# A two-layer gated cross-attention kernel: the first head's keys and queries laid out by TensorE instead of by way of memory, and the mask summed by GpSimd inside the loop

## The reference, cut to what matters

```
x = x + tanh(g_xattn[0]) * attention0(layernorm(x), ctx)        # 16 heads of 8 channels, no mask
x = x + tanh(g_ffn[0])   * top-2 gated experts0(layernorm(x))   # 8 experts, gelu
x = x + tanh(g_xattn[1]) * attention1(ctx, layernorm(x), mask)  # 16 heads, mask
x = x + tanh(g_ffn[1])   * top-2 gated experts1(layernorm(x))   # 8 experts, silu gate
```

## Time and profile before

| what | value |
|---|---|
| median of 3 runs | 2676.83 us (2675.81 to 2679.16) |
| the profiled execution's own time | 2674.73 us |
| its span, first to last instruction | 2672.7 us |
| mean granted TensorE clock in it | 0.949 |
| TensorE busy / VectorE / ScalarE / GpSimd | 93% / 81% / 72% / 1% |
| first max unit's reduction starts at | 74.37 us |
| the loop over the first head's steps starts at | 195.16 us |

### The profile page before, as it was taken

The page is one execution under the profiler, slowest core; times in us unless marked ns, Lnnn a source line. Parts: engine busy times, 40 slices in busy tenths (PEclk is TensorE's granted clock), DMA queues, the critical chain, the costliest instruction groups (busy, mean ns, idle before and its releaser), DMA issues.

```text
span 2672.7 us, 50522 instructions
## 1 busy us (share of the span) xinstructions
PE 2493.9 (93%) x20890; PEld 952.0 (36%) x20892; DVE 2156.5 (81%) x2215; ACT 1935.6 (72%) x3545; POOL 27.6 (1%) x27
## 2 busy tenths in 40 slices
PE   2379999999999999999796899999999999999989
PEld 1243333333333333334342333333333333333343
DVE  5469999999999999953536899999999999999144
ACT  2058888888888888885331388888888888888932
POOL 4000000000000000000000000000000000000000
PEclk8559999999999999999896799999999999999989
DMA  7120000000000000003100000000000000000000
GB/s 251 69 82 21 29 29 29 29 29 29 29 28 28 28 29 29 23 24 109 65 0 22 6 29 28 28 28 28 29 29 29 29 29 28 28 28 14 1 0 8
DMA packets 36415, 94.33 MB, mean 35 GB/s; under 512 B 4020, under 2 KB 14808, under 8 KB 35928
## 3 DMA queue, kind: packets, MB, share of 16 engines
q1 hardware_dynamic: 34744, 90.69, 9.4%
q10 hardware_dynamic: 1440, 0.40, 0.1%
HBM read 75.08 MB, written 15.74 MB: 34 GB/s over the span
## 4 chain that ended last, share of the span: by engine, by line
PE 63%; DVE 31%; SPq 2%; DMA 1%; issue 1%; ACT 1%; DVEq 0%; ACTq 0%
DVE m_part L657 28%; PE ps L978 22%; PE ps L930 19%; PE ps L949 10%; PE ps L1076 4%; PE ps L1084 3%; SPq L299 1%; PE ps L890 1%; PE ps L920 1%; DMA probs<-in_mask_t 1%; PE ps L882 1%; DVE probs L613 1%; SPq L308 1%; PE ps L1096 1%; DMA k_parts<-probs 1%
## 5 line engine op out<-in xcount | busy, mean ns | idle before, releaser
L657 DVE TENSOR_REDUCE m_part<-ps 128x2 f32<-128x1024 f32 (+1 forms) x1664 | 1932.5, 1184 | 166.9 <-PE ps L949 162.3
L495 ACT ACTIVATE probs<-ps 128x512 f32<-128x512 f32 (+1 forms) x3264 | 1759.5, 595 | 314.3 <-PE ps L930 194.9
L978 PE MATMUL ps<-probs,v_all 128*9 128x256 f32 x13056 | 1013.0, 382 | 1.7 <-ACT o_raw L475 0.5
L930 PE MATMUL ps<-q_ring,k_ring 35*128 35x512 f32 x3264 | 872.6, 497 | 0.6 <-ACT q_ring L484 0.4
L949 PE MATMUL ps<-k_ring,q_ring 33*128 33x512 f32 (+1 forms) x3328 | 732.3, 419 | 62.5 <-DVE m_part L657 36.2
L930 PEld LDWEIGHTS ps<-q_ring,k_ring 35*128 35x128 f32 x3264 | 347.9, 183 | 712.9 <-ACT probs L495 618.3
L949 PEld LDWEIGHTS ps<-k_ring,q_ring 33*128 33x128 f32 x3328 | 348.9, 193 | 150.6 <-DVE m_part L657 108.7
L978 PEld LDWEIGHTS ps<-probs,v_all 128*9 128x9 f32 x13056 | 194.4, 88 | 551.5 <-ACT probs L495 472.8
L794 DVE TENSOR_TENSOR probs<-probs,ps 128x512 f32<-128x512 f32 x64 | 39.7, 683 | 74.5 <-ACT probs L528 70.1
L528 ACT ACTIVATE probs<-ps,b_col 128x512 f32<-128x512 f32 x64 | 44.0, 687 | 70.2 <-PE ps L1076 70.2
L678 DVE RECIPROCAL r_den<-ps 128x8 f32<-128x8 f32 x32 | 6.6, 207 | 107.0 <-PE ps L957 106.7
(11 more groups left out here) (127 smaller groups left out, 576.1 us busy)
## 6 DMA issues: line engine op xcount, KB each, us to landing
k_ring<-k_parts SPq DMA_DIRECT2D x384, 96.0 KB
k_ring<-k_parts SPq DMA_DIRECT2D x128, 112.2 KB
probs<-in_mask_t SPq DMA_DIRECT2D x10, 640.0 KB, 4.4
k_parts<-probs SPq DMA_DIRECT2D x12, 512.0 KB, 3.1
k_parts<-big SPq DMA_DIRECT2D x12, 512.0 KB, 3.1
q_ring<-q_parts SPq DMA_DIRECT2D x120, 32.0 KB
big<-in_w SPq DMA_DIRECT2D x1, 2048.0 KB, 10.7
q_parts<-probs SPq DMA_DIRECT2D x4, 512.0 KB, 3.5
```

The costliest lines, as they stand in the source:

```text
L495: A(probs[0:k, n % PSLOTS, HALF * half:HALF * half + HALF], ps[0:k, e_bank(unit), :], ACT.Exp, scale=SCALE).then_inc(sem(f"exp_done{l}"), 1)
L657: V.tensor_reduce(m_part[:, h % 2, :, p, c], mx(n % 2)[:, :, 0:chunk_w[c]], AX.X, ALU.max).then_inc(sem(f"mx_done{l}"), 1)
L930: pe.matmul(bank, k_ring[row:row + ROWS_EXP, koff:koff + P], q_ring[row:row + ROWS_EXP, qoff:qoff + HALF], start=not masked, stop=True).th ...
L978: mm = pe.matmul(ps[32 * g:32 * g + VW, 7, 0:QGW], v_all[:, t, h, :], probs[:, n % PSLOTS, QGW * g:QGW * g + QGW], start=(t == 0), stop=(t ...
```

## The change

- **The first head, layer 0.** Its rows no longer come through memory. After a chunk's keys are projected and split, TensorE multiplies them with two small selection matrices (`repeat`), which puts the 8 channels on their 64 rows of a PSUM bank, and ScalarE copies that bank into `k_ring` and adds the ones by a bias column (`copy_over`). The queries go the same way, with four matmuls. Three chunks are projected ahead; the other ten are projected between the first head's own max units, as are the repeats.
- **Who splits.** ScalarE evacuates each key chunk twice (rounded, and as it is), and GpSimd forms the low part (`low_keys`), not VectorE. `k_st` and `q_st` of layer 0 now lie in the second slot of `k_ring`.
- **The mask.** GpSimd adds the 11 pieces as 32-bit words (`put_mask_together`) after its work on the keys; VectorE reduces the folded remainder before layer 1. ScalarE's `sum_mask` is gone, and the stage has moved to the `spare` part of `big`.
- **SyncE's queue.** Order: x, ctx, queries' store, key stores 0 to 2, queries of head 1, key group 0 of head 1, the other key stores, key groups 1 to 3 of head 1 (after all 14 copies), queries of head 2, then `setup`, then `check_mask`, then `load_heads`. The first head's eight query and sixteen key transfers are gone.
- **GpSimd's start.** The long memsets are gone from it: selection matrices first, then (after the layer norm) short memsets, `low_keys`, the constants that VectorE waits for (`rank`) after the third chunk, and the ones of the second slot in two parts (`set_ones`).
- **Small things.** The rows unit is a matmul by a rounded identity, not a transpose; `keep_warm` runs four times in each of the two steps before the first `weigh`, and the dense steps are eight, not four, in both layers; one buffer for the row biases; the values have one PSUM bank and stand one unit earlier; one table function (tanh) moved behind the first maxima.

The diff, cut to its core:

```diff
 def dense(h, t):
 
-    return 3 if h == 0 and t < 4 else 0
+    return 3 if h == 0 and t < 8 else 0
 K_GROUPS = [(0, 3), (3, 6), (6, 9), (9, KCH)]
+UPPER = 6
+
+
+REPEATS = [0, "q"] + list(range(1, KCH))
+REPEAT_AT = {u: n for n, u in enumerate(REPEATS)}
+RING_SET = KRING + 2
+MASK_LEFT = 160
...
-        k_st = [of[:, 0:KST * PARTS * HALF].bitcast(F32R).rearrange("p (a b w) -> p a b w", a=KST, b=PARTS)
-                for of in (flat3(probs)[:, 2 * TQ:], spare)]
+        sum_stage = [spare[:, n * MCH * TQ // 4:(n + 1) * MCH * TQ // 4] for n in range(2)]
+        k_st = [of[:, 0:KST * PARTS * HALF].rearrange("p (a b w) -> p a b w", a=KST, b=PARTS)
+                for of in (k_ring[:, KW + HALF * UPPER:], spare.bitcast(F32R))]
+        mask_sum = spare[:, KST * PARTS * HALF:KST * PARTS * HALF + MCH * TQ // 4]
+        k_sum = spare[:, TQ:2 * TQ].rearrange("p (a w) -> p a w", a=2)
+        r_at = KW + 2 * PARTS * HALF
+        r_k = k_ring[0:HD, r_at:r_at + PARTS * P].rearrange("p (n r) -> p n r", n=PARTS)
+        r_q = k_ring[0:HD, r_at + PARTS * P:r_at + 3 * PARTS * P].rearrange("p (n r) -> p n r", n=2 * PARTS)
...
             def load_first0():
 
-                sp.wait_ge(sem("ring_set"), RING_SET)
-                first_queries(0)
-                store_k(0)
+                store_q(0)
+                for g, (c0, c1) in enumerate(K_GROUPS):
+                    store_k(0, c0, c1)
+                    if g == 0:
+                        sp.wait_ge(sem("ring_set"), RING_SET)
+                        sp.wait_ge(sem("q_stored0"), 16 * 2)
+                        load_queries(0, 1)
+                        sp.wait_ge(sem("copied_over"), REPEAT_AT["q"] + 1)
+                        keys_stored(0, c1)
+                        load_keys(0, 1, g)
                 keys_stored(0)
-                for g in range(len(K_GROUPS)):
-                    load_keys(0, 0, g)
-                sp.wait_ge(sem("q_stored0"), 16 * 2)
-                load_queries(0, 1)
-                for g in range(len(K_GROUPS)):
+                sp.wait_ge(sem("copied_over"), NCH + 1)
+                for g in range(1, len(K_GROUPS)):
                     load_keys(0, 1, g)
                 load_queries(0, 2)
...
             sp.dma_start(x_sb[:, :, :], a["x"].rearrange("(t p) c -> p t c", p=P)).then_inc(sem("x_in"), 16)
+            load_context()
+            load_first0()
             setup()
-            load_first0()
             check_mask()
...
+                selections()
+                pool.wait_ge(sem("xn_q0"), QT)
                 set_ring()
+
+            def more_constants():
+                link(nc.gpsimd.tensor_scalar(neg_i[:, :], ident_f[:, :], MASKED, 0.0, ALU.mult, ALU.add))
+                link(nc.gpsimd.memset(m_pad[:, :, :].bitcast(F32), 0.0))
+                link(nc.gpsimd.memset(ones_f[:, :], 1.0))
                 for e in range(E):
-                    nc.gpsimd.memset(rank[:, e:e + 1], float(E - e)).then_inc(sem("rank"), 1)
-                nc.gpsimd.memset(ones_f[:, :], 1.0).then_inc(sem("rank"), 1)
-                nc.gpsimd.memset(m_pad[:, :, :], 0.0).then_inc(sem("rank"), 1)
+                    link(nc.gpsimd.memset(rank[:, e:e + 1], float(E - e)))
                 nc.gpsimd.memset(zeros[:, :], 0.0).then_inc(sem("rank"), 1)
-                nc.gpsimd.tensor_scalar(neg_i[:, :], ident_f[:, :], MASKED, 0.0, ALU.mult, ALU.add).then_inc(sem("rank"), 1)
-                pool.wait_ge(sem("rank"), E + 4)
+                pool.wait_ge(sem("rank"), 1)
                 nc.gpsimd.tensor_tensor(pick_e[:, :], ident_f[0:2 * E, 0:E], ident_f[0:2 * E, E:2 * E], ALU.add).then_inc(sem("pick_e"), 1)
+                pool.wait_ge(sem("pick_e"), 1)
+                nc.gpsimd.tensor_scalar(ident_r[:, :], ident_f[:, :], 1.0, 0.0, ALU.mult, ALU.add).then_inc(sem("ident_r"), 1)
+                pool.wait_ge(sem("ident_r"), 1)
```

```diff
+            def low_keys(c):
+
+                w = chunk_w[c]
+                pool.wait_ge(sem("k_evac0"), 2 * c + 2)
+                nc.gpsimd.tensor_tensor(k_st[0][:, c % KST, 1, 0:w], k_sum[:, c % 2, 0:w], k_st[0][:, c % KST, 0, 0:w].bitcast(F32),
+                                        ALU.subtract).then_inc(sem("k_split0"), 1)
+                pool.wait_ge(sem("k_split0"), c + 1)
+
+            def put_mask_together():
+
+                words = mask_sum.bitcast(I32)
+                link(nc.gpsimd.memset(mask_sum, 0.0))
+                for c in range(NFULL // MCH + 1):
+                    pool.wait_ge(sem(f"mask_in{c % 2}"), 16 * (c // 2 + 1))
+                    rows, n = (P, MCH * TQ // 4) if c < NFULL // MCH else (TAIL, TQ // 4)
+                    new = sum_stage[c % 2].bitcast(I32)[0:rows, 0:n]
+                    if c:
+                        pool.wait_ge(sem("mask_met"), c)
+                    nc.gpsimd.tensor_tensor(words[0:rows, 0:n], words[0:rows, 0:n], new, ALU.add).then_inc(sem("mask_met"), 1)
+                pool.wait_ge(sem("mask_met"), NFULL // MCH + 1)
+                n = MCH * TQ // 8
+                while n > MASK_LEFT:
+                    link(nc.gpsimd.tensor_tensor(words[:, 0:n], words[:, 0:n], words[:, n:2 * n], ALU.add))
+                    n //= 2
+                nc.gpsimd.tensor_tensor(words[:, 0:n], words[:, 0:n], words[:, n:2 * n], ALU.add).then_inc(sem("mask_folded"), 1)
 
             constants()
+            for c in range(NCH):
+                low_keys(c)
+                if c == 2:
+                    more_constants()
+                if c == UPPER:
+                    pool.wait_ge(sem("copied_over"), REPEAT_AT["q"] + 1)
+                    pool.wait_ge(sem("q_stored0"), 16 * 2)
+                    set_ones(0, HALF * UPPER, 0)
+            pool.wait_ge(sem("copied_over"), NCH + 1)
+            for n in range(KST):
+                pool.wait_ge(sem(f"k_stored0_{n}"), 16 * len(range(n, NCH, KST)))
+            set_ones(HALF * UPPER, TK, 2)
+            put_mask_together()
...
+            def project_k(c):
+
+                w = chunk_w[c]
+                act.wait_ge(sem("k_proj0"), c + 1)
+                if c >= KST:
+                    act.wait_ge(sem(f"k_stored0_{c % KST}"), 16 * (c // KST))
+                    act.wait_ge(sem("repeated"), REPEAT_AT[c - KST] + 1)
+                A(k_st[0][:, c % KST, 0, 0:w], ps[:, 4 + c % 2, 0:w], ACT.Identity, bias=b_col[:, 0, 1:2]).then_inc(sem("k_evac0"), 1)
+                if c >= 2:
+                    act.wait_ge(sem("k_split0"), c - 1)
+                A(k_sum[:, c % 2, 0:w], ps[:, 4 + c % 2, 0:w], ACT.Identity, bias=b_col[:, 0, 1:2]).then_inc(sem("k_evac0"), 1)
+
+            def copy_over(what):
+
+                act.wait_ge(sem("repeated"), REPEAT_AT[what] + 1)
+                if what == "q":
+                    act.wait_ge(sem("ring_set"), RING_SET)
+                    A(q_ring[:, 0:HALF], ps[:, 6, :], ACT.Identity).then_inc(sem("copied_over"), 1)
+                else:
+                    act.wait_ge(sem("one_rows"), 2)
+                    A(k_ring[:, HALF * what:HALF * what + chunk_w[what]], ps[:, 6, 0:chunk_w[what]], ACT.Identity,
+                      bias=one_rows[:, 0:1]).then_inc(sem("copied_over"), 1)
...
+            project_k(0)
+            project_k(1)
+            project_q(0)
+            copy_over(0)
+            project_k(2)
+            copy_over("q")
+            copy_over(1)
+            for c in range(NCH):
+                if c + 3 < NCH:
+                    project_k(c + 3)
+                if c + 2 < NCH:
+                    copy_over(c + 2)
+                set_v(c)
             act.wait_ge(sem("g_in"), 32)
             A(g_tanh[:, :], g_raw[:, :], ACT.Tanh).then_inc(sem("g_tanh"), 1)
-            act.wait_ge(sem("att_w_in0"), ATT_IN)
-            project_q(0)
-            project_k()
-            for c in range(NCH):
-                set_v(c)
-                if c < NFULL // MCH + 1:
-                    sum_mask(c)
-            act.wait_ge(sem("mask_summed"), NFULL // MCH + 1)
...
                     for c0, _ in CTX_CHUNKS:
                         if c * HALF == c0:
                             pe.wait_ge(sem(f"ctx_in{c0}"), 16)
-                if c >= 2:
-                    pe.wait_ge(sem(f"k_split{l}"), c - 1)
-                pe.matmul(ps[:, c % 2, 0:w], w_att[:, l, 1, :], ctx_t[:, HALF * c:HALF * c + w],
+                if c >= 2 and l == 0:
+                    pe.wait_ge(sem("k_evac0"), 2 * c - 2)
+                if c >= 2 and l == 1:
+                    pe.wait_ge(sem("k_split1"), c - 1)
+                pe.matmul(ps[:, bank + c % 2, 0:w], w_att[:, l, 1, :], ctx_t[:, HALF * c:HALF * c + w],
                           start=True, stop=True).then_inc(sem(f"k_proj{l}"), 1)
```

```diff
+            def repeat(what):
+
+                n = REPEAT_AT[what]
+                pe.wait_ge(sem("selected"), 4 * PARTS)
+                if n:
+                    pe.wait_ge(sem("copied_over"), n)
+                if what == "q":
+                    pe.wait_ge(sem("q_split0"), 2)
```

(58 more changed lines are left out.)

140 lines of the change are left out of this document (70 added, 70 removed).

## The result

The changed kernel took **3258.34 us** (median of 4 runs), the kernel before beside it 2677.99: a ratio of 1.2181, interval 1.2143 to 1.222. Forecast were 2590 us and a range of 2574 to 2624.

A forecast was written before the change was run, and what follows sets the result against it. The page names TensorE, 93% busy, but the first 195 us were read as bound by engines waiting for each other, not arithmetic. Sum: 2674.7 - 89 (earlier loop start) + 8 (queue) - 4 (rows unit) = 2590 us; range 2574 to 2624.

The forecast's parts named there:

- The opening: Layer 0's start up to the first maximum: first reduction at 31 us, before 74.4; range 28 to 36.
- Term 2: The first head's 52 max units in layer 0: 61 us, taking full clock with 3 us lost at the start.
- the half-clock rival: First head's stage: TensorE stays at 1.2 GHz, 87.5 us instead of 61, kernel at 2616 us; chance 0.20.
- the rise at 50 to 54: Old key stage: clock rose from 0.50 to 0.80 behind back-to-back projections; taken as evidence against the half clock.
- the 79%: Old first stage: TensorE said to be 79% busy through 112 us at 0.50; taken as evidence for the half clock.
- Term 3: The eight units of head 1 before the loop: 14 us, 14.6 before; the loop then starts at 106, not 195.
- VectorE was not held by GpSimd: Rival, first stage: GpSimd's low parts and ones hold up VectorE's reductions, 27 us more, 2617 us; chance 0.06.
- Term 4: SyncE's queue: head 2's keys land at +65 against a need at +57 from loop start, a new wait of +8 us.
- slower than before: Rival, SyncE's queue: head 2's keys behind GpSimd's adds; needs a wait above 98 us, 13.6 us per piece; chance 0.02.
- Term 6: The loop's additional keep_warm fillers: cost 2.7 us a layer, return 3 to 4 us by the clock; 0 in sum.
- Term 5: The rows unit in the loop, a one-pass matmul for four transposes: -4 us, ends -8 and +8.

The follow-up runs named there:

- experiment 1: The changed kernel with the mask's pieces queued one behind each head's loads, not all ahead of head 2's keys: 2615.82 us, ratio 0.9753.
- experiment 2: The changed kernel, queue untouched, with three keep_warm in each of seven steps around and behind the wait for head 2's keys: 2628.82 us, ratio 0.98.
- experiment 3: The kernel before with 2 MB weight reloads queued ahead of head 2's keys: three 2673.8 us, three and a half 3318.07, four 3325.88, five 3329.61.
- experiment 8: The changed kernel with the mask's pieces one behind each head's loads and the loop's fillers of before: 2615.14 us, ratio 0.9758.
- experiment 4: The kernel before without any keep_warm fillers in either layer's loop: 3341.22 us, one execution.
- experiment 5: The changed kernel with its wait, and three more keep_warm in each of eight steps of head 3, some 110 steps later: 2721.31 us, one execution.
- Experiment 6: The changed kernel with three keep_warm in steps around the wait, those behind it feeding 9 rows, not 128: 3255.06 us, one execution.
- experiment 9: The changed kernel with mask pieces one behind each head's loads, a full-row matmul in first-stage units, and the loop's old fillers: 2599.25 us, ratio 0.9697.

## Why the prediction was wrong, point by point

**The opening** was right. The changed kernel's timeline (start, us, engine, line, operation):

```profile
7.79 0.17 DVE L718 TENSOR_SCALAR var_e<-mv 128x8 f32<-128x8 f32 x1
...
8.48 2.14 DVE L722 TENSOR_SCALAR probs<-x_sb,mv,r_std 128x128 f32<-128x128 f32 x8
...
14.30 3.54 PE L987 MATMUL ps<-ctx_t,w_att 128*128 128x512 f32 x4 [14.30 <-DMA b_col<-in_bk]
...
32.43 1.23 DVE L762 TENSOR_REDUCE m_part<-ps 128x2 f32<-128x1024 f32 x1 [9.26 <-PE ps L1080]
```

0.17 for 0.2, the weights at 14.30 for 14.2, the first reduction at 32.43 for 31. The lost microsecond and a half is in the first matmuls: the first key chunks took 3.54 us for two where the earlier trace rows have 1.88. That the clock did this is not shown, since the profile reads 1.00 up to 24 us.

**Term 2** took the wrong clock. The 52 units lasted 83.2 us (32.43 to 115.59), near the half-clock rival's 87.5, not 61. I read the rise at 50 to 54 in the earlier trace rows as a sign for the new stage. What stood ahead of that rise was a row of projections of 128 rows; in the new stage such work is thinned out between units of 33. That this is the reason is not shown: the same stage read 1.00 in 64 to 72 and was back at 0.50 from 76 on. Nor did the old stage bear the 79% that I gave it: TensorE was busy 59.16 of the 112 us from 68 to 180, and 78 to 80% only outside its holes. The chunk at half clock is 7.75 us, one period of this timeline:

```profile
45.02 2.07 PE L987 MATMUL ps<-ctx_t,w_att 128*128 128x512 f32 x2
...
47.74 1.22 PE L1005 MATMUL ps<-k_ring 8*128 8x512 f32 x2
...
48.89 1.22 PE L1080 MATMUL ps<-k_ring,q_ring 33*128 33x512 f32 x4
...
50.04 2.07 PE L1014 MATMUL ps<-w_att,ctx_t 128*128 128x128 f32 x8
```

That the stage is bound by TensorE then, at 7.3 us in the text, was right. At full clock the text has 3.7 us of TensorE in a chunk; the trace has TensorE busy 7.72 of 8 us there, and a chunk of 4.83 (values at 64.47 and 69.30). So 61 us would have held at full clock, but with TensorE as full as VectorE. **Term 3** was 15.6 us for 14; the loop starts at 131.17, where the half-clock rival has 132.5. VectorE was not held by GpSimd: its 1.23 us for a maximum stands throughout.

**Term 4** is the step that failed, not in the wait that it foresaw but in what it charged for it. Due 57 us behind the loop's start, the keys let TensorE go on at +62.2 (forecast +65). SyncE's queue issued them from 182.99 us on, right behind the mask's last piece at 182.66. The low parts took 1.27 us (forecast 1.2), and each of the adds this, of GpSimd's timeline:

```profile
157.27 2.93 POOL L495 TENSOR_TENSOR big<-big 128x1280 int32<-128x1280 int32 x1 [1.25 <-DMA big<-in_mask_t]
```

2.93 for 3.0. What failed is the line "+8 us": the wait was priced at its own length and the steps behind it at their old pace. Experiments 1 to 3 show the missing term: behind 6.0 us of wait, 638 us more for layer 0's loop at half clock. My rival "slower than before" sat at the right place, the same queue, and its point of decision was wrong for the same reason: I asked for a wait of 98 us, and 3.93 were enough in experiment 3. The earlier trace rows had the warning. They have 0.50 through the old first stage and 0.54 at the loop's start, and the loop of before is at full clock later; I never asked what brings it back.

**Term 6** is the same failure seen from the other side. I let the fillers return 3 to 4 us at most. Their extra number is worth nothing (experiment 8), but in layer 0 of the one execution without any the loop stood at half clock, some 665 us (experiment 4), and the ones that the change had stood ahead of the new wait, where they could not undo its fall; behind it they did (experiments 2 and 5). The Trainium skill, page TensorE: Matmul & The Clock Gate, section "What's actually happening", ties the clock to how busy TensorE has been. The trace agrees with the fall in a wait. It does not agree with the loop: busy 1500.00 of 1500 us by the profile, it stayed at 0.50, and it did so in experiments 3, 4 and 6 as well.

**Term 5** was -0.5 us in layer 1 by experiment 8, not -4 in sum: a gain too small to tell. **The sum with the measured clock:** without the wait the change is worth 2616 us (experiment 1), which is the half-clock rival's own number (though that had 8 us of wait in it). Had I only got the stage's clock right, 2616 would have stood inside the range. It is the wait that takes the result out of it.

Not settled: which property of the work the chip goes by. Experiment 6 separates 9 rows from 128 and no more, and its rows lie in the moving and the stationary operand alike. Rows alone can't be the answer: the loop's own `weigh` matmuls (L1109) are 128*9 like the full fillers, in f32 for bf16, and with 5560 of them between 200 and 1700 the clock stayed at 0.50. Padding the loop's own operands was not tried. Nor is it settled when full-row matmuls act: in experiment 9 they stood in the stage for 34 us at 0.50.

## What to carry to other kernels

Price a new wait of the engine that sets the time by the clock it comes out with, not by its length: find in the old profile where that clock fell and what was running when it rose again, and ask whether this work exists behind the new wait. If a loop of thin matmuls shows 1.00, look for what put it there, and try a few full-row matmuls behind each place at which TensorE may stand idle; then read the clock in several executions, since experiments 4 and 9 show the same code in either state. Where a page shows TensorE busier after a change, with longer matmuls of the same shape, as here, read the clock row first.

## What the runs showed of the hardware

- A loop of matmuls with 33 or 35 rows, or with 128 rows and 9 columns, in use, TensorE busy 100% by the profile, kept a granted clock of 0.50 for 1500 us and, started at 1.00, kept 1.00 for over 900 us. In the traces here neither state ended inside the loop's regular steps without a wait or fillers.
- Idle stretches of 3.93, 5.84, 5.97, 6.00, 8.21 and 16.16 us were each followed by the low state in that loop; in the shortest one it read 0.61 in the stretch that began 1.5 us behind the last matmul.
- Twelve full-row matmuls in each of seven or eight steps ended the low state of the loop in both places tried (steps 43 to 49, some 22 us behind the wait; steps 155 to 162, some 12 us behind the first of them). With 9 rows, the same number at nearly the same duration (401 for 419 ns) did not, in one execution.
- The same start of the loop, with no fillers and gaps of 0.38 and 0.40 us, fell to 0.50 in layer 0 and stayed at 1.00 in layer 1 of one execution (experiment 4).
- At half clock the loop's matmuls take 1.56 to 1.61 times as long, not twice.
- GpSimd's add of two 128 x 1280 int32 inputs takes 2.93 us, 2.3 ns an element. The Trainium skill's GPSIMD Engine Reference, under "Elementwise — side-by-side cycle accounting", has 4497 ns for a float add of 2048 elements, by which the estimate was 2.8 us: the trace agrees, for an integer add.
